# Attention inside a fused block: folding two masked score triangles into one, two transposes a head instead of three, and the normalisation on ScalarE

## The reference, cut to what matters

```
qkv = hidden @ W_pack              # 16 query heads, 8 key heads, 8 value heads of 128
q, k = rope(q), rope(k)
k, v = conv2(k), conv2(v)          # two taps along the sequence
mask = (j <= i) & (i - j < 128)    # causal, window of 128
probs = softmax(where(mask, q @ k.T / sqrt(128), min))
out = (probs @ v) @ W_o
```

## Time and profile before

| | |
|---|---|
| median of 3 runs | 758.59 us |
| the profiled execution | 757.21 us |
| its span | 755.4 us |
| TensorE busy | 727.5 us (96%) |
| VectorE busy | 531.0 us (70%) |
| ScalarE busy | 464.7 us (62%) |
| GpSimd busy | 429.9 us (57%) |
| mean granted TensorE clock | 0.990 |

### The profile page before, as it was taken

The page is one execution under the profiler, slowest core; times in us unless marked ns, Lnnn a source line. Parts: engine busy times, 40 slices in busy tenths (PEclk is TensorE's granted clock), DMA queues, the critical chain, the costliest instruction groups (busy, mean ns, idle before and its releaser), DMA issues.

```text
span 755.4 us, 12879 instructions
## 1 busy us (share of the span) xinstructions
PE 727.5 (96%) x4144; PEld 624.1 (83%) x4144; DVE 531.0 (70%) x1554; ACT 464.7 (62%) x1273; POOL 429.9 (57%) x339
## 2 busy tenths in 40 slices
PE   8799999999999999999999999999999989999996
PEld 6598889988899998889999888999877857777875
DVE  5898897689876868987686797778664225454383
ACT  5788868777986776788677678777553212222110
POOL 3545445454465588646548864655545507567356
PEclk9999999999999999999999999999999989999998
DMA  8960007600005011000401102040369889996772
GB/s 303 322 139 1 2 0 241 230 0 2 1 1 192 5 49 48 33 1 1 166 2 48 40 28 76 3 168 1 124 166 258 220 267 263 289 228 71 171 226 84
DMA packets 62418, 84.44 MB, mean 112 GB/s; under 512 B 6376, under 2 KB 50293, under 8 KB 62352
## 3 DMA queue, kind: packets, MB, share of 16 engines
q1 hardware_dynamic: 52240, 70.59, 30.4%
q0 software_dynamic: 7680, 8.95, 6.2%
q10 hardware_dynamic: 2432, 4.07, 1.5%
HBM read 54.81 MB, written 33.51 MB: 117 GB/s over the span
## 4 chain that ended last, share of the span: by engine, by line
PE 76%; DVE 12%; ACT 6%; issue 2%; DMA 2%; POOL 1%; ACTq 0%; POOLq 0%; DVEq 0%
PE PJ L1386 22%; PE OUT L1520 9%; PE U L1505 6%; PE U L1465 6%; PE U L1672 5%; PE U L1494 4%; PE U L1464 3%; PE U L1506 3%; PE U L1620 2%; PE U L1386 2%; PE XB L1691 2%; PE OUT L1691 2%; PE OUT L1620 2%; PE XB L1386 2%; ACT U L570 1%
## 5 line engine op out<-in xcount | busy, mean ns | idle before, releaser
L792 POOL TENSOR_TENSOR qsw<-qsw,sinT 128x512 f32<-128x512 f32 x95 | 125.7, 1323 | 167.4 <-ACT qsw L557 166.5
L1017 DVE CUSTOM_DVE_ANT_0 U<-U,mask 128x128 f32<-128x128 f32 (+1 forms) x256 | 86.6, 379 | 50.8 <-PE U L1465 50.4
L570 ACT ACTIVATE U<-U,nmax 128x128 f32<-128x128 f32 (+1 forms) x256 | 100.4, 392 | 32.0 <-DVE nmax L1017 31.5
L1386 PE MATMUL PJ<-hT_hi,w_hi 128*128 128x512 f32 x254 | 110.8, 436 | 1.1 <-issue 1.1
L1386 PE MATMUL PJ<-hT_lo,w_hi 128*128 128x512 f32 x254 | 100.4, 395 | 0.0
L1386 PE MATMUL PJ<-hT_hi,w_lo 128*128 128x512 f32 x254 | 100.2, 394 | 0.0
L796 POOL TENSOR_TENSOR qr<-qr,qsw 128x512 f32<-128x512 f32 x64 | 82.6, 1291 | 29.0 <-DVE qr L1001 28.4
L556 ACT ACTIVATE qsw<-PJ 64x512 f32<-64x512 f32 x96 | 57.1, 594 | 51.7 <-PE PJ L1386 42.3
L803 POOL DMA_INDIRECT slot_rows<-xn,sidx x64 | 64.8, 1012 | 40.8 <-issue 13.1
L1520 PE MATMUL OUT<-wo_hi,oT_hi 128*128 128x256 f32 x256 | 82.9, 324 | 1.4 <-DVE wo_lo L1041 1.2
L1034 DVE TENSOR_TENSOR oT_lo<-U,oT_hi 128x256 fp32r<-128x256 f32 x128 | 54.1, 423 | 37.4 <-ACT oT_hi L577 37.2
(11 more groups left out here) (227 smaller groups left out, 1837.1 us busy)
## 6 DMA issues: line engine op xcount, KB each, us to landing
wgu<-in_dram SPq DMA_DIRECT2D x32, 352.0 KB, 9.7
expert_sum<-blank SPq DMA_DIRECT2D x3, 2176.0 KB, 17.5
slot_rows<-blank SPq DMA_DIRECT2D x1, 4624.0 KB, 26.5
late_sums<-expert_sum SPq DMA_DIRECT2D x9, 512.0 KB, 8.9
wd_a<-in_dram SPq DMA_DIRECT2D x12, 352.0 KB
wraw<-in_dram SPq DMA_DIRECT2D x8, 512.0 KB, 8.7
bcm<-mod_rows SPq DMA_DIRECT2D x8, 512.0 KB, 6.8
xe<-slot_rows ACTq DMA_DIRECT2D x10, 289.0 KB, 6.7
```

Source lines behind the costliest of these rows:

```text
L570: last = act.activation(U[n % 3][:, a:z], U[n % 3][:, a:z], ACT.Exp, scale=-1.0, bias=nmax[:, n % 4, j:j + 1], accum_out=rsum[:, n % 4, j: ...
L792: pool.tensor_tensor(pair3(qsw[:, n % NQSW, :]), pair3(qsw[:, n % NQSW, :]), both(sinT[:, :]), ALU.mult).then_inc(t2_done, 1)
L1017: last = dve.tensor_tensor_reduce(out=U[n % 3][:, a:z], in0=U[n % 3][:, a:z], in1=allowed, scale=-float(HD) ** -0.5, scalar=3.4e38, op0=AL ...
L1386: last = pe.matmul(out_ap, a(c), b_(c), start=(n == 0), stop=(n == len(steps) - 1))
```

## The change

The window triangle of the second queries' scores (columns 128 to 255 of the bank) is copied into the block of the causal one (columns 256 to 383), where the causal mask forbids. From there on the second queries have one block of 128 columns instead of two, all of it allowed. So the scores' minimum, the exponential and the normalisation see 128 columns for each half. `prob` has two blocks, and TensorE makes two transposes. The transposed second block is unfolded by one masked copy on VectorE (`masked`), which writes the window part into the second block of `pT` and the causal part into its third; the places that it does not write stay zero from the start. The normalisation itself moves from VectorE to ScalarE (two copies with a scale per partition), behind `transposed(n-1)` in its queue; VectorE keeps the reciprocal.

```diff
-            for dst, src in ((mask[:, :], mask_t[:, PN:3 * PN]), ...
+            for dst, src in ((mask[:, PN:2 * PN], mask_t[:, 0:PN]), ...
...
             def exps_of(n):
                 act.wait_ge(sneg_done, n + 1)
-                for j, (a, z) in enumerate(((0, PN), (PN, 3 * PN))):
+                for j, (a, z) in enumerate(((0, PN), (2 * PN, 3 * PN))):
...
-                act.activation(pT[:, n % 2, :], U[n % 3][:, 0:3 * PN], ACT.Copy).then_inc(pt_done, 1)
+                act.activation(pT[:, n % 2, 0:PN], U[n % 3][:, 0:PN], ACT.Copy).then_inc(norm_done, 1)
+
+            def normalise(n):
+                act.wait_ge(rinv_done, n + 1)
+                for j, a in enumerate((0, 2 * PN)):
+                    last = act.activation(prob[:, n % 2, j * PN:(j + 1) * PN], U[n % 3][:, a:a + PN], ACT.Copy,
+                                          scale=rinv[:, n % 4, j:j + 1])
+                last.then_inc(norm_done, 1)
...
                 if 0 <= n - 1 < NU:
                     transposed(n - 1)
+                if 0 <= n < NU:
+                    normalise(n)
...
+            pool.memset(pT[:, :, PN:3 * PN], 0.0).then_inc(fills, 1)
+            pool.memset(mask[:, 0:PN], 0.0).then_inc(fills, 1)
...
                 dve.wait_ge(sc_ps, n + 1)
-                for j, (a, z, allowed) in enumerate(((0, PN, mask[:, PN:2 * PN]), (PN, 3 * PN, mask[:, :]))):
-                    last = dve.tensor_tensor_reduce(out=U[n % 3][:, a:z], in0=U[n % 3][:, a:z], in1=allowed,
+                bank = U[n % 3]
+                dve.copy_predicated(bank[:, 2 * PN:3 * PN], mask[:, PN:2 * PN].bitcast(I32), bank[:, PN:2 * PN]).then_inc(dve_own, 1)
+                own.n += 1
+                folded = own.n
+                for j, (a, allowed) in enumerate(((0, mask[:, PN:2 * PN]), (2 * PN, mask[:, 0:PN]))):
+                    if j == 1:
+                        dve.wait_ge(dve_own, folded)
+                    last = dve.tensor_tensor_reduce(out=bank[:, a:a + PN], in0=bank[:, a:a + PN], in1=allowed,
...
-            def normalise(n):
+            def inverse_sums(n):
                 dve.wait_ge(exp_done, n + 1)
-                dve.reciprocal(rinv[:, n % 4, :].rearrange("p (j k) -> p j k", k=2),
-                               rsum[:, n % 4, :].unsqueeze(2).broadcast_to([PN, 2, 2])).then_inc(rinv_done, 1)
-                dve.wait_ge(rinv_done, n + 1)
-                dve.tensor_tensor(prob[:, n % 2, :].rearrange("p (j k) -> p j k", k=PN),
-                                  U[n % 3][:, 0:3 * PN].rearrange("p (j k) -> p j k", k=PN),
-                                  rinv[:, n % 4, 1:4].unsqueeze(2).broadcast_to([PN, 3, PN]), ALU.mult).then_inc(norm_done, 1)
+                dve.reciprocal(rinv[:, n % 4, :], rsum[:, n % 4, :]).then_inc(rinv_done, 1)
+
+            def masked(n):
+
+                dve.wait_ge(norm_done, 2 * (n + 1))
+                dve.copy_predicated(pT[:, n % 2, PN:3 * PN].rearrange("p (k q) -> p k q", k=2), parts[:, :, :].bitcast(I32),
+                                    U[n % 3][:, PN:2 * PN].unsqueeze(1).broadcast_to([PN, 2, PN])).then_inc(pt_done, 1)
...
                 if 0 <= n < NU:
-                    normalise(n)
+                    inverse_sums(n)
+                if n == 0:
+                    own(dve.tensor_tensor(parts[:, 1, :], tri[:, :], ident[:, :], ALU.add))
+                    own(dve.tensor_scalar(parts[:, 0, :], parts[:, 1, :], -1.0, 1.0, ALU.mult, ALU.add))
+                if 0 <= n - 1 < NU:
+                    masked(n - 1)
...
             def p_transpose(n):
-                pe.wait_ge(norm_done, n + 1)
-                for j in range(3):
+                pe.wait_ge(norm_done, 2 * n + 1)
+                for j in range(2):
                     last = pe.transpose(U[n % 3][:, j * PN:(j + 1) * PN], prob[:, n % 2, j * PN:(j + 1) * PN], ident[:, :])
```

More of the change, by code:

```diff
@@ L114, in adaln_block @@
         rows8.close()
-        prob = sb("prob", [PN, 2, 3 * PN], F32, att)
+        parts = sb("parts", [PN, 2, PN], F32, att)
+        prob = sb("prob", [PN, 2, 2 * PN], F32, att)
         pT = sb("pT", [PN, 2, 3 * PN], F32, att)
@@ L125, in adaln_block @@
         rsum = sb("rsum", [PN, 4, 2], F32, att)
-        rinv = sb("rinv", [PN, 4, 4], F32, att)
+        rinv = sb("rinv", [PN, 4, 2], F32, att)
         st1 = sb("st1", [PN, TT, 6], F32, att)
@@ L372, in _ @@
             w_load(W_ORDER[W_FIRST])
-            for dst, src in ((mask[:, :], mask_t[:, PN:3 * PN]), (tri[:, :], tri_t), (ebase[:, :], ebase_t),
+            for dst, src in ((mask[:, PN:2 * PN], mask_t[:, 0:PN]), (tri[:, :], tri_t), (ebase[:, :], ebase_t),
                              (wnorm[:, :], w_norm.partition_broadcast(PN))):
@@ L1250, in _ @@
             w_low(W_FIRST - 1)
-            dve.wait_ge(fills, 10)
+            dve.wait_ge(fills, 12)
             dve.wait_ge(ld_rope, 64)
```

## The result

The changed kernel takes 766.74 us, the median of 4 runs (764.33 to 771.42), against 757.60 for the kernel before (755.42 to 761.98): a ratio of 1.0135, 95% interval 1.0097 to 1.0172. It is slower by 1.0 to 1.7%. The profiled execution took 764.33 us with a span of 762.5 us; the granted clock was 0.991 (before 0.990).

The account below looks back on a forecast made before the run. TensorE's queue was taken to set the pace in nearly all 128 steps. The sum -14.1 + 4.3 + 12.9 - 1.5 + 0.4 = +2.0 on 757.2 us, with the runs' median 1.4 above, gave 760 us; range 746 to 774.

Parts of the forecast that it names:

- slower: Outcome class for the whole kernel: a measured time above 766 us, chance 0.3.
- the likeliest class: Outcome class for the whole kernel: within 1% of the kernel before, covering forecast and third rival, chance 0.5.
- the unfolding copy was not dear: Rival on VectorE: unfolding copy at 0.56 us, fold dearer too, some 60 steps stall 0.2 more: 772 us, chance 0.3.
- TensorE was not the bound everywhere: Rival: TensorE stays the bound everywhere, the waits shrink to 2 us: 746.5 us, chance 0.2.
- The prices: Per instruction: VectorE's fold 0.295 us and unfolding copy 0.42, ScalarE's scaled copy 0.34, TensorE's transpose 0.11.
- The new wait on ScalarE: normalise waits for VectorE's reciprocal: ScalarE idles 0.44 us in ordinary steps, 1.2 with k_conv, some 80 in all.
- The moved wait on TensorE: weighted_v waits for VectorE's unfolding copy: margin 0.10 us in k_conv steps, 14 of 32 over it, +4.3 us.
- The stretch: Steps 71 to 81: no gain over 46.96 us, where TensorE alone would win 1.2.
- The gain on offer: TensorE loses one transpose a unit, 128 x 0.11 = 14.1 us, only as far as TensorE stays the bound.
- the hook stretches: Steps where ScalarE's hooks make it late: 12.9 us lost over the four passes, less 1.5 counted already.
- The first pass: Pass 1 of the hook stretches, with nine weight splits of about 1.06 us on ScalarE: 4.3 us lost.

Follow-up runs that it names:

- two reorderings: Changed kernel with ScalarE's normalise behind its hooks and, in k_conv steps, VectorE's reciprocal and unfolding copy ahead of V's second tap: 748.14 us, ratio 0.9893.

## Why the prediction was right, and where it was off

The measured time lies inside the range, at 6.7 us above the forecast, and at 1.35% it falls into "slower", which had 0.3, not into the likeliest class. The range was 28 us wide, and that is what held it; the net was forecast at +2.0 us, and by the start of step 127 the changed kernel is 9.9 us behind. What was right is the mechanism of the two waits and where they would stand. No single rival describes it: the unfolding copy was not dear, and TensorE was not the bound everywhere.

- **The prices** held. The fold took 290 ns (taken: 295), the unfolding copy 427 (0.42), a scaled copy 364 where I went by a row of 339. TensorE's step fell from 3.74 to 3.63 us. By the Trainium skill, "ScalarE: Activation LUTs", section "What ACT_TABLE_LOAD costs", a scaled copy would take an estimated 386 ns; the measured 364 lies between that and my row.
- **The new wait on ScalarE** is there with its sizes: 0.29 us in ordinary steps (0.44 forecast), 1.02 with the key convolution (1.2), 61 us in all (80). It ends when it should: in step 73 the scaled copies begin 334.83 - 333.29 = 1.54 us after `oT_hi`, forecast 1.58. A bare ScalarE step is 3.75 - 0.46 of hooks = 3.29 us; forecast 3.30.
- **The moved wait on TensorE**: the copy in step 59 ends 0.46 us behind the start of the next step, forecast 268.66 - (268.26 - 0.11) = 0.51 (without the 0.05 to its waiter). The waits for it sum to 23.2 us, 18.5 above L1505's before. I charged 4.3 us of time for this wait; without the copy and its wait the kernel is 6.5 us faster.
- **The stretch** of steps 71 to 81 takes 48.23 us; I said it would gain nothing over 46.96.
- **The gain on offer** is the term that was mis-sized. I set it at 14.1 us, "only as far as TensorE stays the bound", and took back only what the change itself makes late. One transpose less on the kernel before gives 4 us. The trace of before already showed the reason. "Nearly all" steps were to have one of the two lengths, 3.74 and 4.19; within 0.05 us it is 89 of 127. In the others, steps 39 to 42 of the run and their like in later passes above all, TensorE waits for VectorE, and a shorter TensorE waits longer there. With 4 in place of 14.1 the sum would be +12.1 us, above the 9.1 measured, so part of what I charged for the hook stretches was this same loss.
- **The first pass** is the second. I charged 4.3 us against a gain of 32 x 0.11 = 3.5. It came out 6.0 us behind. With the nine weight splits ahead of `normalise` the loss is 2.1, with all other work too 1.1. So it matters that they stood in ScalarE's queue behind a wait. The wait itself is not longer there: 12.1 us in this pass, 15.8 to 17.2 in each later one. Which part of the 6.0 us I failed to count beyond that is not shown.

That two reorderings, which change no instruction, give back 18 us shows that the loss is one of order in two queues, not one of work. That the two halves are ScalarE's lateness and the copy's is argued from where each acts; each edit shifts both waits somewhat.

## What to carry to other kernels

When a change moves an operation to another engine, look first at what the operation waits for and at what stands behind it in its new queue. Here a wait of 0.3 to 1.0 us a unit ahead of all hooks cost 8 to 9 us. Put the waiting instruction behind the work that doesn't need it, as long as its consumer has slack (in the changed kernel the transposes began 1.1 to 1.8 us after `prob` was done in most steps). The same move on VectorE, made in every step, cost time, since there the instruction moved ahead had to wait itself. And before counting a saving on the busiest engine as a gain, try it alone: 14 us of TensorE's time were worth 4 with these queues and 8 to 10 with better ones.

## What the runs showed of the hardware

VectorE's key convolution, both of whose inputs lie in SBUF, has a median of 743 ns and a maximum of 3262 in the changed kernel. Nine of its 32 cases took more than 0.75 us, two of them 3262 ns. In the first of these two GpSimd ran two 512-column additions in SBUF meanwhile:

```profile
303.85 3.26 DVE L1022 SCALAR_TENSOR_TENSOR kc<-kr,cwk,k 128x512 f32<-128x512 f32 x1
```
```profile
304.05 2.51 POOL L824 TENSOR_TENSOR xres<-xres,yg 128x512 f32<-128x512 f32 x2
```
```profile
307.89 0.63 ACT L595 ACTIVATE prob<-U,rinv 128x128 f32<-128x128 f32 x2 [3.53 <-DVE rinv L1042]
```

In eight of the nine cases an addition or product of GpSimd overlapped the convolution, which ended 0.55 to 0.56 us behind the end of such an instruction; the ninth took 0.80 us with none. Of the other 23 only two overlapped one. They kept their 0.74 us, and the addition that began 0.18 us behind their start took 1.70 us, where the same addition took 1.26 to 1.29 otherwise. So one waits for the other, in either direction.

The Trainium skill, "SBUF — State Buffer", section "Who interferes with whom", describes a port pair that VectorE and GpSimd share as an exclusive lock, and says that a VectorE instruction with two SBUF inputs contends with a GpSimd instruction that reads SBUF. The rows agree with it. The unfolding copies, with one input in SBUF and one in PSUM, never took more than 454 ns, though 95 of the 128 overlapped a GpSimd addition or product.

What pays for it is another engine: ScalarE stood 3.53 us for the reciprocal behind that convolution, and step 68 came out 1.8 us longer than before.
